# Embedding lookups and pairwise dot products: both tiles' rows transposed by groups among the lookups, both Grams in a row, and most gathers held until they are done

## What is computed

```python
e = stack([tbl_f[ids[:, f]] for f in range(27)], axis=1)   # (2048, 27, 128), fp32
dot = einsum('bnd,bmd->bnm', e, e)                         # Gram of 27 rows for each sample
z = dot's 351 entries with i < j                           # (2048, 351)
h = concatenate([z, dense_ctx], axis=1)                    # 16 more
h = maximum(h @ W_top1 + b_top1, 0)                        # 512
h = maximum(h @ W_top2 + b_top2, 0)                        # 256
y = h @ W_top3                                             # (2048, 1)
```

## Time and profile before

| | us |
|---|---|
| runs of the kernel | 508.52, 509.54, 524.95; median 509.54 |
| the profiled execution | 509.38 |
| its span, first to last instruction | 507.6 |

### The profile page before, as it was taken

How to read it: one execution, slowest core, us unless ns; L and a number is a source line. 1 busy time by engine, 2 the same in 40 slices (tenths; PEclk the granted TensorE clock), 3 DMA queues, 4 the chain that set the end, 5 groups by cost and what they waited for, 6 DMA issues and landing times.

```text
span 507.6 us, 14911 instructions
## 1 busy us (share of the span) xinstructions
PE 383.8 (76%) x6214; PEld 344.5 (68%) x6214; DVE 234.4 (46%) x505; ACT 131.5 (26%) x165; POOL 272.3 (54%) x264
## 2 busy tenths in 40 slices
PE   1568255797769956699588995699776995799897
PEld 1467144796659945599377985589565884579786
DVE  3676116476317533166332871255631654326441
ACT  2246010233203412033121340122320332212432
POOL 6888745665446455264653744557444556537100
PEclk9969555999779979699877996799878998979999
DMA  6996413122112311212212131132211231111000
GB/s 170 263 261 168 126 32 80 46 64 85 34 36 77 110 41 41 66 35 90 58 35 72 43 105 31 41 75 60 91 36 34 77 109 42 36 27 47 16 1 0
DMA packets 22279, 36.32 MB, mean 72 GB/s; under 512 B 12662, under 2 KB 13310, under 8 KB 22252
## 3 DMA queue, kind: packets, MB, share of 16 engines
q1 hardware_dynamic: 13996, 19.01, 13.3%
q0 software_dynamic: 8256, 16.92, 13.0%
HBM read 35.90 MB, written 0.01 MB: 71 GB/s over the span
## 4 chain that ended last, share of the span: by engine, by line
PE 70%; issue 20%; DVE 4%; DMA 3%; SPq 1%; another core or an unknown queue 1%; ACT 1%; DVEq 0%
PE emb_ps L694 27%; PE gram_ps L739 16%; PE mlp_ps L758 7%; PE emb_ps L730 6%; PE mlp_ps L772 5%; PE emb_ps L710 4%; DMA ids_b<-in_ids_mm 3%; DVE onehot L565 3%; PE mlp_ps L780 2%; PE emb_ps L827 1%; PE mlp_ps L749 1%; PE emb_ps L839 1%; SPq L276 1%; DVE parts L545 0%
## 5 line engine op out<-in xcount | busy, mean ns | idle before, releaser
L421 POOL DMA_INDIRECT rows<-in_tbl,idx x256 | 269.6, 1053 | 198.7 <-PE gram_ps L739 73.7
L694 PE MATMUL emb_ps<-onehot,parts 125*128 125x256 f32 x1280 | 167.7, 291 | 30.8 <-DVE onehot L565 11.8
L694 PEld LDWEIGHTS emb_ps<-onehot,parts 125*128 125x128 f32 x1280 | 160.8, 195 | 34.1 <-ACT parts L441 11.9
L565 DVE TENSOR_SCALAR onehot<-ids_b,row_of 128x512 fp32r<-128x512 int32 x320 | 131.4, 483 | 75.3 <-PE emb_ps L694 51.8
L739 PE MATMUL gram_ps<-embT 128*32 128x26 f32 x4096 | 82.2, 221 | 85.9 <-issue 84.5
L739 PEld LDWEIGHTS gram_ps<-embT 128*32 128x32 f32 x4096 | 67.4, 141 | 103.9 <-issue 102.1
L587 DVE STREAM_TRANSPOSE turned<-gram_ps 128x832 f32<-128x832 f32 x16 | 16.8, 1050 | 152.3 <-PE gram_ps L739 152.3
L453 ACT ACTIVATE embT<-emb_ps 128x512 f32<-128x512 f32 x40 | 48.9, 1236 | 122.4 <-PE emb_ps L694 89.2
L461 ACT ACTIVATE embT<-emb_ps 128x512 f32<-128x512 f32 x32 | 36.7, 1243 | 96.3 <-PE emb_ps L730 96.3
L581 DVE COPY embT<-emb_ps 128x512 f32<-128x512 f32 x32 | 35.6, 1184 | 10.8 <-PE emb_ps L730 10.3
L758 PE MATMUL mlp_ps<-zT,w_sb 128*128 128x256 f32 (+1 forms) x168 | 38.7, 378 | 0.0
(11 more groups left out here) (40 smaller groups left out, 107.8 us busy)
## 6 DMA issues: line engine op xcount, KB each, us to landing
ids_b<-in_ids_mm SPq DMA_DIRECT2D x8, 896.0 KB
ids_b<-in_ids_mm SPq DMA_DIRECT2D x16, 256.0 KB
rows<-in_tbl,idx POOLq DMA_INDIRECT x256
embT<-in_tbl SPq DMA_DIRECT2D x6, 448.0 KB
w_sb<-in_tbl SPq DMA_DIRECT2D x2, 448.0 KB
turned<-in_tbl SPq DMA_DIRECT2D x1, 560.0 KB
w_sb<-in_W_top SPq DMA_DIRECT2D x1, 512.0 KB
turned<-in_tbl SPq DMA_DIRECT2D x1, 448.0 KB
```

Of the source, the lines that this page charges most:

```text
L421: pool.indirect_dma_start(rows[:, t, n, :], None, tables[f], bass.IndirectOffsetOnAxis(idx[:, t, f:f + 1], 0), engine_sem=gathers_written) ...
L565: last = nc.vector.tensor_scalar(onehot[:, k % OH:k % OH + LOOK_TABLES, c, :], ids_b[:, k:k + LOOK_TABLES, :], row_of[:, c:c + 1], None, A ...
L694: last = nc.tensor.matmul(emb_ps[BANK[k]][:, m * W:(m + 1) * W], parts[0:MP, f, part, c * D:(c + 1) * D], onehot[0:MP, f % OH, c, :], star ...
```

## The change

- TensorE's order becomes: lookups 0, 1, 2 (with z of the pair before after lookup 0), half of the first layer, group 0 of both tiles, the other half of the first layer, lookup 3, group 1, lookup 4, X, group 2, half of the second layer, group 3, the other half, then both Grams in a row.
- The jobs are renumbered to suit (`LOOK_JOB`, `XJOB`, `ROW_JOB`); ScalarE moves all rows of tile 0 and VectorE all rows of tile 1.
- The second Gram gets a PSUM place of its own, the upper two of the four banks, so the wait of a Gram for the `flip` is dropped; lookup 2 waits for it.
- `keep_step` is removed. Gathers go group by group for both tiles. After the first 3 of a pair's 32 (`EARLY`) GpSimd waits until both Grams of the pair before are done, then issues the other 29 with no further wait of that kind. The first pair has no such wait.
- The indices come in two buffers, each holding both tiles: one is used for group 0, the other for the rest.
- ScalarE and VectorE take the new order; in the first pair their splits of tables are interleaved with it.
- TensorE begins with 110 increments of an unused semaphore (`PE_PAD`).

```diff
-XJOB = LOOK
+LOOK_JOB = [0, 1, 2, 5, 8]
+XJOB = 9
+ROW_JOB = [[3, 4], [6, 7], [10, 11], [12, 13]]
-BY_DVE = (LOOK + 1) * [0] + TILES * [0, 1, 0, 1]
+BY_DVE = [int(any(k == jobs[1] for jobs in ROW_JOB)) for k in range(JOBS)]
-CALLS_AFTER = [{3: 6}, {3: 8}]
+EARLY = 3
+PE_PAD = 110
+IDX = [range(0, 1), range(1, NT)]
...
-        emb_ps = [ps(f"emb_ps{k}", [P, 512]) for k in range(EMB_BANKS)]
-        gram_ps = ps("gram_ps", [P, G * COLS])
+        emb_all = ps("emb_ps", [P, EMB_BANKS * 512])
+        emb_ps = [emb_all[:, k * 512:(k + 1) * 512] for k in range(EMB_BANKS)]
+        gram_own = ps("gram_ps", [P, G * COLS])
+        gram_ps = [gram_own[:], emb_all[:, EMB_BANKS * 512 - G * COLS:]]
...
+            def gather(p, t, k, at):
+                for m, n in enumerate(TR[k]):
+                    if not isinstance(p, int) or p:
+                        if k == t == 0 and m == EARLY:
+                            pool.wait_ge(gram_filled, p * TILES)
+                            pool.sem_inc(pool_waited, 1)
+                    f = GATHERED[n]
+                    one_queued(at + m)
+                    pool.indirect_dma_start(rows[:, t, n, :], None, tables[f],
...
+                for h, groups in enumerate(IDX):
+                    pool.wait_ge(s_idx[h], (p + 1) * 16)
+                    pool.sem_inc(pool_waited, 1)
+                    for k in groups:
+                        if k == 0:
+                            past(pool, emb_filled, (p - 1) * JOBS + row_job(TILES - 1, k) + 1)
+                            pool.sem_inc(pool_waited, 1)
+                        for t in range(TILES):
+                            gather(p, t, k, at + (k * TILES + t) * len(TR[k]) + (TILES if first and k > 1 else 0))
...
             def emb_moved(p, t):
-                done = [row_job(t, k) for k in range(NT)]
-                wait_moved(pe, p, max(j for j in done if BY_DVE[j]))
-                wait_moved(pe, p, max(j for j in done if not BY_DVE[j]))
+                wait_moved(pe, p, row_job(t, NT - 1))
+            def body(p, first):
+                def rows_of(k):
+                    for t in range(TILES):
+                        transpose_rows(p, t, k)
+                lookup(p, 0)
+                if not first:
+                    transpose_z(p - 1, 1)
+                lookup(p, 1)
+                if not first:
+                    pe.wait_ge(s_turned, p * TILES)
+                lookup(p, 2)
...
+                    for call in range(2 * KCH):
+                        first_layer(p - 1, 0, call)
+                rows_of(0)
+                for call in range(0 if first else 2 * KCH):
+                    first_layer(p - 1, 1, call)
+                lookup(p, 3)
+                rows_of(1)
+                lookup(p, 4)
+                if first:
+                    transpose_x()
+                else:
+                    lookup_x(p)
+                rows_of(2)
+                for call in range(0 if first else N1):
+                    second_layer(p - 1, call)
+                rows_of(3)
+                for call in range(N1, N1 if first else N1 * N2):
+                    second_layer(p - 1, call)
                 for t in range(TILES):
                     gram(p, t)
                 if not first:
                     third_layer(p - 1)
...
+            for _ in range(PE_PAD):
+                pe.sem_inc(pe_begun, 1)
             sweep_alike(pe, body)
```

More of the change, by code:

```diff
@@ L85, in row_job @@
 def row_job(t, k):
-    return LOOK + 1 + t * NT + k
+    return ROW_JOB[k][t]
 NJ = NF - 1
@@ L306, in _ @@
             sp.sem_inc(s_out, 16)
-            load_idx(0, 0)
-            load_idx(0, 1)
+            for h in range(len(IDX)):
+                load_idx(0, h)
             load_ids(0, 0)
@@ L350, in body @@
                 if not last:
[L351 to L361, removed]
+                    gathered(p, 0)
+                    load_idx(p + 1, 0)
+                    ids_read(p, 2)
+                    load_ids(p + 1, 2)
+                    gathered(p, 1)
+                    if first:
+                        sp.wait_ge(s_x, 16 * TILES)
+                    load_idx(p + 1, 1)
                 if not first:
@@ L409, in body @@
-            def body(p, first, last):
[L410 to L432, removed]
@@ L502, in _ @@
             act.sem_inc(mlp_moved, BANKS)
[L504 to L507, removed]
             def body(p, first):
[L510 to L515, removed]
-                move_x(p)
[L517 to L524, removed]
+                if first:
+                    for k in range(7):
+                        split_high(k)
+                    move_lookup(p, 0)
+                    move_lookup(p, 1)
+                    split_high(7)
+                    move_lookup(p, 2)
+                    move_rows(p, 0, 0)
+                    split_high(8)
+                    split_high(9)
+                else:
+                    move_lookup(p, 0)
+                    layers(p - 1, 0)
+                    move_lookup(p, 1)
+                    move_lookup(p, 2)
+                    layers(p - 1, 1)
+                    move_rows(p, 0, 0)
+                    layers(p - 1, 2)
+                move_lookup(p, 3)
+                move_rows(p, 0, 1)
+                move_lookup(p, 4)
+                move_x(p)
+                move_rows(p, 0, 2)
+                if first:
+                    split_x_high()
+                move_rows(p, 0, 3)
                 if not first:
+                    layers(p - 1, 3)
                     layers(p - 1, 4)
@@ L616, in _ @@
             dve.wait_ge(s_row, 1)
[L618 to L627, removed]
[L628 to L635 removed]
+            def body(p, first, last):
+                if first:
+                    make_two(p, 0)
+                    split_low(0)
+                    split_low(1)
+                    make_two(p, 2)
+                    split_low(2)
+                    make_two(p, 4)
+                    split_low(3)
+                    make_two(p, 6)
+                    split_low(4)
+                    split_low(5)
+                    make_two(p, 8)
+                    split_low(6)
+                    move_rows(p, 1, 0)
+                    split_low(7)
+                    split_low(8)
+                    split_low(9)
+                    move_rows(p, 1, 1)
+                else:
                     flip(p - 1, 1)
```

124 lines of the change are left out of this document (46 added, 78 removed).

## The result

The changed kernel takes 595.1 us (median of 4 runs, 590.9 to 601.8) against 517.3 us for the kernel before beside it (508.5 to 527.1). Both medians take in slow runs; the means of the fast runs alone are 593.7 and 509.0 us, a ratio of 1.166 with a 95% interval of 1.145 to 1.188: slower by 17%. The forecast was 478 us, faster; the time is even beyond that of rival B, 536 us. The profiled execution took 590.9 us, its span is 589.0 us.

What follows compares the result with a forecast made beforehand. Gathers in flight were taken to starve TensorE and stall the Grams. First pair 61, six pairs of 57.5, last pair 54 and tail 15.8 gave 476, plus 1.8 beyond the span: 478 us, range 428 to 522.

Steps and rivals of the forecast that it cites:

- rival B: Lookups under the long train: supply stays at 1.8 records per us, 66 us a pair, 536 us in all; chance 14%.
- Gathers starve TensorE; the Grams are stalled by them: Grams beside gathers: 11.4 and 9.7 us against 2.36 us each without; moving them saves 16.4 us a pair.
- The store of 57 records: TensorE under a train of gathers: about 57 matmul records run before it stalls, then only a small supply.
- The supply of 3.5 per us: TensorE before the Grams: 3.5 records per us after the store, so 211 of 263 records run by 45 us.
- The 4.6: Upper end of the supply, per us, from 134 matmuls in a 16.7 us train of 12 gathers; 52 us a pair.
- The 1.8: Lower end of the supply, per us, from the stretch 133.3 to 143.0 us with VectorE mostly idle; 66 us a pair.
- 57.5 us a pair: Each of the six middle pairs: 57 us from train, remaining records, two Grams and moves, 57.5 with small gaps.
- The first pair, 61 us: First pair: from 88.4 to 61 us, a gain of 27, bounds 57 to 68; its train ends at 51.
- The last pair, 54 us: Last pair: from 43.1 to 54 us, a loss of 11, with 29 gathers beside it instead of 16.
- The increments cost nothing, -3.5 to +3.5 us a pass: 110 increments at TensorE's start: 1 to 9.9 us, hidden; shifted loop placement -3.5 to +3.5 us for seven passes, taken as 0.
- the 20 us stretch at 1.9 per us: Stalled stretch in the kernel before: 38 records in 20.0 us, cited as evidence for the low supply of rival B.
- Rival A: Lookups aren't starved and the train alone binds: 50 us a pair, last pair 47.5, 426 us in all; chance 28%.

## Why the prediction was wrong, point by point

- *Gathers starve TensorE; the Grams are stalled by them.* Right on the occasions where the kernel before takes 509 us. The kernel with plain transfers shows it: the same order, the same bytes in 32 transfers in a row, 382 us instead of 593. (The 32 in a row of the forecast didn't come: the 3 early gathers wait for the first rows' transposes, and in the second pair they start at 129.6, 14 us after the 29.) The Grams fell from 21 to 4.5 us a pair (2 x 2.7 forecast). In five of the seven sets of measurements (the one with the result counted) the premise doesn't hold: nothing is starved there.
- *The store of 57 records.* Right in the second and the third pair, where the first stall came after 62 records, at +8.2 and +9.0 us. In the last pair TensorE ran 114 records in the first 15.8 us of the train before it stalled. So a fixed store doesn't describe all trains.
- *The supply of 3.5 per us.* **This is the step that failed.** It was interpolated between 1.8 and 4.6 by VectorE's share of the time. In the first of the trains it was (80 - 57)/37.7 = 0.6, in the last 2.1. By 45 us some 211 records should have run; 80 to 141 had run at a train's end. Neither end was a supply for this load. The 4.6 came from a train in which TensorE was busy all 16.70 us: it got all that it asked for, so the number says nothing of a shortage. The 1.8 was taken from the stalled stretch alone; by the sum that gave 4.6, the window named beside it gives (69 - 57)/9.7 = 1.2. And it was a rate of Gram records. Stalled lookups get less, at a similar share of VectorE's time; the kernel before among its Grams, the changed one among its lookups:

```profile
50.30:70.30 20.00, 4.34 (x38) 2.99 (x38) 1.49 (x1) 0.27 (x1) 13.70 (x14) 0.52 0.37 101
88.00:115.00 27.00, 5.84 (x15) 4.12 (x16) 1.92 (x5) 0.49 (x1) 20.28 (x23) 0.57 0.22 54
```

  That is 1.9 per us against 0.6, with VectorE busy 7% of the time in both. So VectorE's share, by which the 3.5 was chosen, doesn't set the rate by itself; the traces above speak against it too, and no experiment on a starving occasion tested it. Why lookups get so few stays open. The forecast also put some 22 us of VectorE's work into the train; 4.8 to 14.4 us fell there, since VectorE waits for TensorE to free one-hots.
- *57.5 us a pair.* 71.8 us measured, six times 14.3 us = 86 us. Check by the same sum: the train ends at 38 us, and TensorE is free 2 us later; of 263 records some 100 have run; 163 x 0.122 = 20 us, transposes and layers 6 us more, Grams 4.5 us: 71 us.
- *The first pair, 61 us.* 78.5 us. The 34 gathers ended at 57.9, not at 51, since several of them took 2 to 4 us in the crowded start, and the first Gram began at 64.5. It stalled under the three early gathers as forecast, and the second one had issue gaps of 1.1 and 1.5 us with no gather beside it, in the first pass of its code. 17.5 us off.
- *The last pair, 54 us.* 63.9 us, by the same supply.
- *The increments cost nothing, -3.5 to +3.5 us a pass.* They took 17.7 us together, more than the 9.9 us that the forecast allowed at most, and so were not hidden under the wait of 10.39 us; most of the 7.3 us was made up later. By the single runs the kernel with them is 8 or 40 us faster, so the change without them would have been slower still.
- *Rival B.* Its mechanism is the one that came true, with its place and its sign: issue gaps at the lookups and a lower clock there (0.63 to 0.82 in the trains). Its price, 66 us a pair, was too low: after the store the first trains got 0.6 per us, not 1.8. Its chance of 14% was too low: the 20 us stretch at 1.9 per us was the nearest row to a long train, and I had set it against a train of 16.7 us in which TensorE never ran short.
- *Rival A* is what happens on the other kind of occasion, at 50 to 51 us a pair from the fourth on; there the kernel before is faster than the prediction could know, since its profile showed only the one kind. The Trainium skill (Runtime: NRT & Kernel Launch, Instruction fetch mechanics) has it that fetching is mostly hidden. The prediction held the starved Grams against that rule, but this doesn't follow. In the profile of the kernel before no 16 KB fetch runs from 275 to 490 us, where Grams stall as before, and none in the starved trains of the changed kernel from the fourth pair on. Where such fetches do run, gaps of 1.7 to 2.6 us stand in the Grams of the second pair and of the kernel without increments.

## What to carry to other kernels

A buffer that hides a shortage turns into a cliff when the same load is put in one piece: count how long the store lasts (here 57 matmuls or more) against the longest train. Don't take the rate behind it from a stretch in which the engine got all that it asked for, nor from another kind of work. A rate that goes with a second engine's busy time proves nothing where that engine waits for the starved one. And holding all of a resource's work back until a stage is done exposes it at the next stage's start, even where nothing is starved: here 455 us against 391.

## What was not expected of the hardware

- The same program took 501 to 527 us in two sets of runs and 389 to 413 us in five others, and the other kernels with indirect gathers went with it, set by set. It isn't a matter of the chip alone: the runs carry a chip number, and number 8 stands beside 508.6 us in one set and beside 396.4 and 391.3 us in two later ones. What differs between them no trace shows.
- While 29 indirect gathers of 64 KB run in a row, TensorE can fall to one matmul in 0.7 to 2.8 us with nothing to wait for, though the DMA share is only 0.20 to 0.27 and the instruction queue brings no code. 32 plain transfers of the same size from the same queue don't do this (busy 24.34 of 24.8 us).
- 110 increments of an unused semaphore ahead of a loop went with 13 code fetches of 16 KB where 39 and 30 were seen without them. The kernel before, unchanged, had 12, 21 and 30.
